# A recurrent block and a mixture-of-experts gate on one core: six blocks in a loop turn instead of two

## The chip, the core and the metric

The kernel runs on one core of one Trainium2 chip. The metric is the device time of one execution in microseconds (us). The core has five engines that run their own instruction streams: TensorE (PE, matmuls; its weight loads are shown as PEld), VectorE (DVE), ScalarE (ACT), GpSimd (POOL) and SyncE (SP), which here issues all DMA transfers. They meet through semaphores alone. The loop of this kernel is a hardware loop: every engine has its own copy of it, with its own counter and its own branch back, and no barrier joins them.

## What is computed

The input `x` is 4 batches of 4096 tokens of 512 values. After a layer normalization, two branches are computed and multiplied, and the product is added to `x`:

```python
xn = _layernorm(x)
# branch 1, on every second token: RMS norm, projection to x_proj and gate, then
def step(h, xt):
    h = jnp.tanh(h * A + xt[:, :, None] * Bm)      # h is (batch 4, 512, 64 states)
    y = h @ c_sum + Dv * xt
    return (h, y)
h_last, ys = jax.lax.scan(step, h0, x_proj)        # 2048 steps, one after the other
s = repeat((ys * silu(gate)) @ w_out.T + b_out, 2)
# branch 2, on every token: encoder 512->1024, sigmoid, controller 1024->64,
# top 2 of 8 experts (64->512->64), 64->1024, sigmoid, decoder 1024->512, layer norm
g = silu(ffn(xn))
out = x + s * g
```

All is in float32. The 2048 steps of the scan are sequential: the state after one is the input of the next.

## The kernel before, in words

The sequence is cut into 64 blocks (`NB`) of 32 steps (`STEPS`), so a block is 64 tokens of each of the 4 batches, and `LAST` is 63. The state is held as 128 partitions by 1024 columns, in two halves `f` of 512 columns. One step of the recurrence takes five kinds of instruction:

- POOL multiplies the broadcast input by `Bm` for both halves into `u`, which has two buffers (line 499, in `step` of the gpsimd function). It waits for `z_ready` of two steps earlier, and every fourth step for a chunk `xb` that SP has loaded (line 410).
- DVE multiplies the state with `A`, `ps_z = h * ps_A`, for each half (line 991), then adds `u` (line 997).
- ACT takes the tanh of each half into the ring `h` (line 601, `tanh`), and DVE's next step waits for it (`h_ready`, line 990).
- PE sums four steps at a time over the states (line 761, `y`).

All other work of a block hangs between the steps. Each engine has a table of slots (`PE_Y`, `PE_DECODE`, `ACT_RELU`, `DVE_DEC_STATS`, `POOL_FIN_SKIP` and so on): a slot of 5 is step 5 of the block itself, one under 0 lies in the block before, one of 32 or more in the block behind. `run_bodies` (line 345) goes through a block's slots and calls `steps` for the recurrence and `between` for the previous, the present and the next block. So the order on each engine is fixed by hand, and in each block an engine also finishes the one before (decoder, output) and prepares the one behind (normalization, projection). These matter below:

- `decode(blk, q)`, lines 892 and 900: the decoder's matmuls, slot 33, thus in slot 1 of the next block. DVE takes their statistics in line 1061 (`dec_stats`, slots 28.75 and 31.75), which wait for the first and the second decode.
- `experts`, lines 845, 857 and 682: expert matmuls on PE and their ReLU on ACT, which stands in ACT's queue between two tanhs.
- `gateT_copy`, line 671: one small ACT instruction in each block, at slot 12.5. It serves here as a mark of where a block is.
- `fin_skip`, line 551, is POOL's last instruction of a turn; `dec_scale`, lines 539 and 541, is POOL's scale for the decoder's norm.

Block 0 is written out, blocks 1 to 62 are 31 turns of a loop with two blocks each (line 358, `eng.Fori`), and block 63 is written out behind. Two is the least that works with buffers and semaphores that alternate by the block's parity. In the loop the number of the block stands in a register, so that counts to wait for are worked out by register instructions; in the blocks written out they are constants:

```python
with eng.Fori(0, (LAST - 1) // 2) as pair:
    body(2 * pair + 1, 1)
    body(2 * pair + 2, 0)
```

In the built program one turn has 229 instructions on SP, 208 on POOL, 460 on ACT, 566 on DVE, and on PE 584, where a matmul is counted once; the profile shows it as four records, two of PE and two of PEld. They are counted from the built program.

Of the kernel before, what the change touches and what calls it, by code (L numbers as in the profile page):

```python
# [43 lines left out]
EH = 512  # L44
T2 = 2 * P
NFILL = 34
LN_EPS = 1e-5
RMS_EPS = 1e-6

# [60 lines left out]
def build(nc, x, w_inT, b_in, A_T, B_T, Cm, Dv, w_outT, b_out, g_norm, W_enc, b_enc, W_s2c, b_s2c,  # L110
          Wr, br, W1, b1, W2, b2, W_c2s, b_c2s, W_dec, b_dec, ln_g, ln_b, out):
    NB = x.shape[1] // (2 * STEPS)
    LAST = NB - 1
# [9 lines left out]
    with ExitStack() as ctx:  # L123
# [145 lines left out]
        def fill_number(blk, k):  # L269

            if isinstance(blk, int) and blk == 0:
                return 4 + k - (2 if k >= FILL_XT else 0)
            if isinstance(blk, int) and blk == LAST:
                return NFILL * blk + 2 + k - (4 if k >= FILL_CONTE else 0)
            return NFILL * blk + 2 + k

        def fill_count(n_or_blk, k):

            if isinstance(n_or_blk, int):
                return fill_number(n_or_blk, k) // 2 + 1  # L280
            return (NFILL // 2) * n_or_blk + (2 + k) // 2 + 1

# [6 lines left out]
        def fin_fill(blk, k):  # L289

            if isinstance(blk, int) and blk == LAST:
                return None, NFILL * (LAST + 1) - 2 + k - FILL_FIN
            return blk + 1, k
# [51 lines left out]
        def run_bodies(eng, steps, between, parts=1):  # L345

            def body(blk, par):
                for n in range(STEPS * parts):
                    slot = n / parts
                    steps(blk, slot)  # L350
                    if not is_first(blk):
                        between(blk - 1, 1 - par, slot + STEPS)
                    between(blk, par, slot)
                    if not is_last(blk):
                        between(blk + 1, 1 - par, slot - STEPS)

            body(0, 0)
            with eng.Fori(0, (LAST - 1) // 2) as pair:
                body(2 * pair + 1, 1)
                body(2 * pair + 2, 0)  # L360
            body(LAST, LAST % 2)
            for n in range(STEPS * parts):
                between(LAST, LAST % 2, STEPS + n / parts)

        def is_first(blk):
            return isinstance(blk, int) and blk == 0

        def is_last(blk):
            return isinstance(blk, int) and blk == LAST
# [3 lines left out]
        def _(sp):  # L373
# [80 lines left out]
            def between(blk, par, slot):  # L454
# [10 lines left out]
                if slot == SP_STORE_OUT:  # L465
                    store_out(blk)

            run_bodies(sp, lambda blk, slot: None, between)
            sp.wait_ge(out_stored, 1 + 16 * QUAD * NB)
            sp.wait_ge(scratch_stored, 16 * QUAD * NB)  # L470
# [5 lines left out]
        def _(pool):  # L476
# [3 lines left out]
            pool.memset(minus_one[:, :], -1.0).then_inc(pool_made, 1)  # L480
            pool.memset(ln_eps[:, :], LN_EPS).then_inc(pool_made, 1)
            pool.memset(rms_eps[:, :], RMS_EPS).then_inc(pool_made, 1)
# [87 lines left out]
            def between(blk, par, slot):  # L570
# [13 lines left out]
                for q in range(2):  # L584
                    if slot == POOL_FIN_ADD[q]:
                        fin_add(blk, q)

            run_bodies(pool, step, between)

        @block.scalar
        def _(act):
# [117 lines left out]
            def between(blk, par, slot):  # L710
# [35 lines left out]
                if slot == ACT_FIN_EVAC:  # L746
                    fin_evac(blk)

            run_bodies(act, tanh, between, parts=F)

# [433 lines left out]
```

## Time and profile before

| what | value |
|---|---|
| median of 3 runs | 6597.48 us |
| lowest and highest run | 6596.17, 6603.51 us |
| span of the profiled execution | 6604.5 us |
| instructions in the profile | 111352 |
| PE, DVE, POOL, ACT busy, share of the span | 94%, 87%, 85%, 60% |
| mean granted TensorE clock, share of full speed | 0.975 |

The profiled execution's own time is not given apart from its span, from the first to the last instruction. The span lies 7.0 us above the median and 1.0 us above the slowest run. The span holds a first stretch in which the weights are loaded, and then 64 blocks of about 102 us. Busy shares are means over all of it. Register, branch and semaphore instructions are not counted as busy; an engine's sequencer that does them shows with a q behind its name (DVEq, POOLq).

### The profile page before, as it was taken

The numbers are of one execution on the slowest core, as the hardware profiler recorded it, in microseconds if no ns is written. First come the engines' busy times: TensorE is split into PE (matmuls) and PEld (weight loads), VectorE is DVE, ScalarE is ACT, GpSimd is POOL, SyncE is SP. The second block draws the span as 40 slices with busy tenths as digits, with TensorE's granted clock in tenths as the row PEclk, the third lists the DMA queues.
The fourth block names the chain that finished last, engine by engine and source line by source line (L and its number), as shares of the span: only waits on it lengthen the run. The fifth ranks groups of instructions, "written<-read, shape, count | busy, mean of one in ns | idle before, by whom it ended". The sixth has DMA issues, their size and how long they took to land.

```text
span 6604.5 us, 111352 instructions
## 1 busy us (share of the span) xinstructions
PE 6237.1 (94%) x29376; PEld 3229.9 (49%) x29376; DVE 5737.4 (87%) x10060; ACT 3984.4 (60%) x8390; POOL 5612.7 (85%) x3276
## 2 busy tenths in 40 slices
PE   5999999999999999999999999999999999999998
PEld 3554445445544454454444544445444545444454
DVE  4988889888898888988888888889888898888887
ACT  3666566566565665656656656566566665565665
POOL 4888888888888888888888888888888888888887
PEclk9999999999999999999999999999999999999999
DMA  5443444444444444444344444444444444434443
GB/s 138 104 108 92 104 109 98 106 101 101 105 98 102 100 97 106 103 97 110 93 105 101 100 106 98 103 106 96 105 101 100 106 98 103 106 95 105 103 100 83
DMA packets 158032, 675.52 MB, mean 102 GB/s; under 512 B 45589, under 2 KB 46613, under 8 KB 91799
## 3 DMA queue, kind: packets, MB, share of 16 engines
q1 hardware_dynamic: 157336, 667.24, 41.6%
q8 instruction: 315, 5.16, 0.3%
q14 instruction: 381, 3.12, 0.2%
HBM read 616.73 MB, written 50.33 MB: 101 GB/s over the span
## 4 chain that ended last, share of the span: by engine, by line
POOL 54%; issue 29%; PE 13%; DVE 1%; POOLq 1%; SPq 1%; ACT 1%; DMA 0%; DVEq 0%; ACTq 0%
POOL u L499 46%; PE bank L845 3%; POOL g L545 2%; PE ps_y L761 2%; PE ps_acc L857 2%; PE bank L794 1%; PE bank L781 1%; POOL gt L532 1%; POOL d_r L541 1%; PE bank L900 1%; PE ps_acc L900 1%; POOL conte L551 1%; PE bank L921 1%; POOL p_r L515 1%; SPq L375 1%
## 5 line engine op out<-in xcount | busy, mean ns | idle before, releaser
L499 POOL TENSOR_TENSOR u<-xb,bt 128x1024 f32<-128x1024 f32 x2048 | 4832.9, 2366 | 789.2 <-DVE ps_z L997 782.8
L601 ACT ACTIVATE h<-ps_z 128x512 f32<-128x512 f32 x4096 | 2374.7, 601 | 1691.8 <-DVE ps_z L997 1587.5
L991 DVE TENSOR_TENSOR ps_z<-h,ps_A 128x512 f32<-128x512 f32 x4096 | 2674.1, 691 | 517.3 <-ACT h L601 329.2
L997 DVE TENSOR_TENSOR ps_z<-ps_z,u 128x512 f32<-128x512 f32 x4096 | 2660.7, 691 | 39.6 <-POOL u L499 37.3
L845 PE MATMUL bank<-wide,w 65*128 65x256 f32 x4096 | 1141.2, 404 | 1.9
L761 PE MATMUL ps_y<-h,c_wide 128*32 128x512 f32 x8192 | 1007.1, 610 | 80.4 <-ACT h L601 80.4
L794 PE MATMUL bank<-xnT,w_enc 128*128 128x256 f32 x4096 | 922.4, 384 | 49.5 <-DVE g L1082 42.6
L845 PEld LDWEIGHTS bank<-wide,w 65*128 65x128 f32 x4096 | 700.2, 189 | 449.8 <-issue 320.2
L794 PEld LDWEIGHTS bank<-xnT,w_enc 128*128 128x128 f32 x4096 | 772.4, 191 | 256.9 <-issue 81.0
L682 ACT ACTIVATE hT<-bank 128x512 f32<-128x512 f32 x1024 | 604.0, 598 | 383.8 <-PE bank L845 366.4
L857 PE MATMUL ps_acc<-hT,w 128*64 128x256 f32 x4096 | 668.7, 405 | 6.6
L761 PEld LDWEIGHTS ps_y<-h,c_wide 128*32 128x32 f32 x8192 | 216.3, 110 | 615.2 <-issue 416.3
L900 PE MATMUL bank<-w_dec,wide 128*128 128x512 f32 x1024 | 480.3, 624 | 0.0
L900 PE MATMUL ps_acc<-w_dec,wide 128*128 128x512 f32 x1024 | 456.6, 599 | 0.0
L781 PE MATMUL bank<-w_in,xnT 128*128 128x512 f32 x1024 | 453.9, 597 | 0.0
L857 PEld LDWEIGHTS ps_acc<-hT,w 128*64 128x64 f32 x4096 | 202.5, 134 | 357.2 <-issue 296.8
L900 PEld LDWEIGHTS bank<-w_dec,wide 128*128 128x128 f32 x1024 | 199.1, 200 | 286.4 <-issue 286.4
L900 PEld LDWEIGHTS ps_acc<-w_dec,wide 128*128 128x128 f32 x1024 | 189.7, 190 | 262.4 <-issue 262.4
L921 PE MATMUL bank<-w_out,conte 128*128 128x512 f32 x512 | 313.9, 770 | 0.0
L624 ACT ACTIVATE wide<-bank,b_enc_col 128x256 f32<-128x256 f32 x512 | 213.9, 471 | 148.1 <-PE bank L794 148.1
L781 PEld LDWEIGHTS bank<-w_in,xnT 128*128 128x128 f32 x1024 | 191.4, 192 | 216.8 <-issue 216.5
L665 ACT ACTIVATE conte<-ps_acc,gate 128x64 f32<-128x64 f32 x1024 | 226.5, 369 | 0.0
(107 smaller groups left out, 4324.6 us busy)
## 6 DMA issues: line engine op xcount, KB each, us to landing
xb<-x_proj_scratch SPq DMA_DIRECT2D x2048, 256.0 KB, 4.3
xbuf<-in_L_attn_x SPq DMA_DIRECT2D x256, 128.0 KB
xres<-in_L_attn_x SPq DMA_DIRECT2D x512, 64.0 KB
out<-g SPq DMA_DIRECT2D x256, 128.0 KB
x_proj_scratch<-xp SPq DMA_DIRECT2D x256, 64.0 KB
w_in<-in_L_attn_w_in SPq DMA_DIRECT2D x1, 2048.0 KB
w_enc<-in_L_ffn_W_enc SPq DMA_DIRECT2D x1, 2048.0 KB
w_dec<-in_L_ffn_W_dec SPq DMA_DIRECT2D x1, 2048.0 KB
```

The costliest lines, as they stand in the source:

```text
L499: pool.tensor_tensor(u[:, tau % 2, :, :], xt, bt[:, :, :], ALU.mult).then_inc(u_ready, 1)
L601: act.activation(h[:, tau % RING, f, :], ps_z[:, f, :], ACT.Tanh).then_inc(h_ready, 1)
L682: drained(act.activation(hT[:, n % 2, :], bank[n % 2][:, :], ACT.Relu), at)
L761: ins = pe.matmul(ps_y[32 * j:32 * j + 32, :], c_wide[:, f, SP - 4 - 4 * k:2 * SP - 4 - 4 * k], h[:, (QUAD * k + j) % RING, f, :], start=( ...
L781: ins = pe.matmul(bank[half][:, :], xnT[:, par, k, 0, :], w_in[:, k, D * half:D * half + D], start=(k == 0), stop=(k == KD - 1))
L794: ins = pe.matmul(bank[n % 2][:, T2 * half:T2 * half + T2], w_enc[:, k, P * m:P * m + P], xnT[:, par, k, :, :], start=(k == 0), stop=(k == ...
L845: ins = pe.matmul(bank[n % 2][:, T2 * half:T2 * half + T2], w_1[0:MA, e, P * t:P * t + P], conteT[:, e, :], start=True, stop=True)
L857: ins = pe.matmul(eo_acc[M * half:M * half + M, :], w_2[:, 4 * (n // 2) + t, :], hT[:, n % 2, T2 * half:T2 * half + T2], start=(n == 0 and ...
L900: ins = pe.matmul(dst[:, :], wide[:, k, P * q:P * q + P], w_dec[:, k, :], start=False, stop=(k == KH - 1))
L921: ins = pe.matmul(bank[1][:, :], oT[:, k, :], w_out[:, k, :], start=False, stop=(k == KD - 1))
L991: dve.tensor_tensor(ps_z[:, f, :], h[:, (tau - 1) % RING, f, :], ps_A[:, f, :], ALU.mult).then_inc(m_done, 1)
L997: dve.tensor_tensor(ps_z[:, f, :], ps_z[:, f, :], u[:, tau % 2, f, :], ALU.add).then_inc(z_ready, 1)
```

## The change

A constant `TURN = 6` is added, and the loop holds six blocks in a turn. With `LAST` at 63 there are 62 // 6 = 10 turns, for blocks 1 to 60. Blocks 61 and 62 are then written out behind the loop, and 63 as before, so three stand there. Parities are the same as before, since 6 is even. Nothing else changes: no slot, buffer, semaphore or operation.

```diff
+TURN = 6
...
             body(0, 0)
-            with eng.Fori(0, (LAST - 1) // 2) as pair:
-                body(2 * pair + 1, 1)
-                body(2 * pair + 2, 0)
+            turns = (LAST - 1) // TURN
+            with eng.Fori(0, turns) as turn:
+                for j in range(TURN):
+                    body(TURN * turn + (1 + j), (1 + j) % 2)
+            for blk in range(TURN * turns + 1, LAST):
+                body(blk, blk % 2)
             body(LAST, LAST % 2)
             for n in range(STEPS * parts):
                 between(LAST, LAST % 2, STEPS + n / parts)
```

In the built program a turn then has 665 instructions on SP, 620 on POOL, 1372 on ACT, 1690 on DVE and 1736 on PE (a matmul again counted once). The code ahead of the loop has the same length on every engine.

PE at the end of a turn, before. Line 879 makes the inputs of the second sigmoid, 892 and 900 are the decoder, 358 is the loop.

```order
L761 MATMUL ps_y<-h,c_wide 32x512 x8
L879 MATMUL bank<-hT,w_c2s 128x256 x4
L879 MATMUL ps_acc<-hT,w_c2s 128x256 x2
L309 REGISTER_ALU
L879 MATMUL bank<-hT,w_c2s 128x256 x2
L358 REGISTER_ALU
L358 COMPARE_AND_BRANCH
```

PE in the change between the second and the third block of a turn, where the turn ended before (lines are 4 higher within the engines' functions).

```order
L765 MATMUL ps_y<-h,c_wide 32x512 x8
L883 MATMUL bank<-hT,w_c2s 128x256 x4
L883 MATMUL ps_acc<-hT,w_c2s 128x256 x2
L310 REGISTER_ALU
L883 MATMUL bank<-hT,w_c2s 128x256 x2
L760 REGISTER_ALU
L765 MATMUL ps_y<-h,c_wide 32x512 x8
L896 MATMUL bank<-bias_rows,ones 128x512
```

The order of the matmuls is the same; the loop's register instruction and branch are gone from this joint, and the sum `y` and the decoder follow at once.

DVE at the end of a turn, before. 997 adds `u`, 1061 takes the statistics of the second decode.

```order
L997 TENSOR_TENSOR ps_z<-ps_z,u 128x512
L324 REGISTER_ALU
L1061 BN_STATS d_st<-ps_acc 128x6
L358 REGISTER_ALU
L358 COMPARE_AND_BRANCH
```

DVE in the change between the second and the third block of a turn.

```order
L1001 TENSOR_TENSOR ps_z<-ps_z,u 128x512
L325 REGISTER_ALU
L1065 BN_STATS d_st<-ps_acc 128x6
L994 ISA
L995 TENSOR_TENSOR ps_z<-h,ps_A 128x512 x2
L999 ISA
```

Here too the branch is gone, and the next block's first step (995) follows behind one register instruction of another kind. The same holds for ACT, POOL and SP.

## Rows read from the trace of the kernel before

**Rows 1.** Waits of DVE: who waited for whom, us in total, times, longest.

```profile
DVE ps_z L991 <- issue: 130.9, 30, 4.9
DVE d_st L1061 <- PE bank L900: 129.6, 34, 7.7
```

**Rows 2.** Line 358 over the span: durations ns min/median/max, first and last start us.

```profile
L358 PEldq COMPARE_BRANCH  x31: 83/3934/4777, 355.0 to 6458.9; - x31
```

**Rows 3.** Line 358 in the stretch 2170 to 2220 us, the end of one turn.

```profile
L358 SPq COMPARE_BRANCH  x1: 45/45/45, 2194.5 to 2194.5; - x1
L358 SPq FUSED_REGOPS  x1: 64/64/64, 2194.8 to 2194.8; - x1
...
L358 POOLq COMPARE_BRANCH  x1: 45/45/45, 2202.3 to 2202.3; - x1
L358 POOLq FUSED_REGOPS  x1: 78/78/78, 2202.6 to 2202.6; - x1
...
L358 DVEq COMPARE_BRANCH  x1: 63/63/63, 2207.2 to 2207.2; - x1
...
L358 ACTq COMPARE_BRANCH  x1: 45/45/45, 2207.8 to 2207.8; - x1
L358 DVEq FUSED_REGOPS  x1: 85/85/85, 2212.3 to 2212.3; - x1
L358 ACTq FUSED_REGOPS  x1: 68/68/68, 2212.7 to 2212.7; - x1
```

**Rows 4.** Line 671 in four stretches: count, ns min/median/max, first and last start us.

```profile
L671 ACT ACTIVATE w<-ps_acc x61: 371/371/372, 224.9 to 6329.9; 8x256 f32<-8x256 f32 x61
L671 ACT ACTIVATE w<-ps_acc x2: 371/372/372, 224.9 to 322.8; 8x256 f32<-8x256 f32 x2
L671 ACT ACTIVATE w<-ps_acc x2: 371/371/371, 6329.9 to 6426.6; 8x256 f32<-8x256 f32 x2
L671 ACT ACTIVATE w<-ps_acc x2: 371/371/371, 6426.6 to 6524.2; 8x256 f32<-8x256 f32 x2
```

**Rows 5.** Busy us (count) of PE, PEld, DVE, ACT, POOL; clock, DMA share, GB/s.

```profile
2257.80:2354.50 96.70, 94.89 (x459) 49.63 (x459) 89.59 (x158) 62.26 (x131) 87.59 (x52) 1.00 0.45 107
2354.50:2462.90 108.40, 101.80 (x460) 51.61 (x459) 89.48 (x158) 62.20 (x132) 87.75 (x52) 0.94 0.39 96
```

**Rows 6.** Waits of PE in 2257.8 to 2354.5 us, the block without a branch.

```profile
PE bank L772 <- DVE g L1099: 1.7, 1, 1.7
```

**Rows 7.** PE in order of time around its branch: start us, us, what [idle before].

```profile
2187.49 3.36 PE L761 MATMUL ps_y<-h,c_wide 128*32 128x512 f32 x16 [2.82 <-ACT h L601]
```

**Rows 8.** PE in order of time at the same place one block earlier.

```profile
2087.88 1.92 PE L761 MATMUL ps_y<-h,c_wide 128*32 128x512 f32 x16
```

**Rows 9.** Busy us of PE (count), clock, DMA share, GB/s, just behind the branch.

```profile
2187.40:2190.60 3.20, 3.11 (x16) 0.52 0.30 98
```

**Rows 10.** DVE in order of time around its branch.

```profile
2207.61 0.69 DVE L1061 BATCH_NORM_STATS2 d_st<-ps_acc 128x6 f32<-128x512 f32 x1
2212.42 1.30 DVE L991 TENSOR_TENSOR ps_z<-h,ps_A 128x512 f32<-128x512 f32 x2 [4.12 <-issue]
2213.62 1.29 DVE L997 TENSOR_TENSOR ps_z<-ps_z,u 128x512 f32<-128x512 f32 x2
```

**Rows 11.** POOL in order of time around its branch.

```profile
2205.73 2.36 POOL L499 TENSOR_TENSOR u<-xb,bt 128x1024 f32<-128x1024 f32 x1
...
2208.83 2.36 POOL L499 TENSOR_TENSOR u<-xb,bt 128x1024 f32<-128x1024 f32 x1
2214.99 2.36 POOL L499 TENSOR_TENSOR u<-xb,bt 128x1024 f32<-128x1024 f32 x1 [3.79 <-DVE ps_z L997]
```

**Rows 12.** Waits of POOL in 2257.8 to 2354.5 us.

```profile
POOL u L499 <- DVE ps_z L997: 8.3, 16, 0.9
```

**Rows 13.** SP's DMA issues in order of time around its branch.

```profile
2204.72 1.82 SPq L410 DMA_DIRECT2D xb<-x_proj_scratch  x4
```

**Rows 14.** The second of two DMA queues that carry instructions: packets, MB, share.

```profile
q14 instruction: 381, 3.12, 0.2%
```

## The prediction

> **What bounds the kernel now.** I read the waits of DVE first. Two of its waits are of the same size and number: 130.9 us in 30 waits before line 991, the first step of a block, with nothing to wait for ("issue"), and 129.6 us in 34 waits for PE's decoder before its statistics [rows 1]. A loop of 31 turns branches back 30 times, so both look like a cost of the turn. The rows of the loop's line show how. The branch itself takes 0.05 to 0.06 us on SP, POOL, DVE and ACT [rows 3]. But the first instruction behind it comes at very different distances: on SP at 2194.8 after 2194.5, on POOL at 2202.6 after 2202.3, that is 0.3 us each; on DVE at 2212.3 after 2207.2, 5.1 us, and on ACT at 2212.7 after 2207.8, 4.9 us [rows 3]. PE shows it in the branch itself: 3.93 us in the median of 31, and 0.083 us in the shortest [rows 2], which I take for the last one, which isn't taken. The two engines that go on at once have the short turns, 229 and 208 instructions; those that stop have 460, 566 and PE's longest. The reading: a branch back to code that is no longer held near the engine waits some 4 to 5 us for it to be fetched.
>
> Next the price of a turn on the whole kernel, from a mark that comes once in a block [rows 4]. From block 1 to block 61 there are 61 marks, so 60 intervals in (6329.9 − 224.9) = 6105.0 us, 30 with a taken branch between the marks and 30 without: 203.5 us a pair. Intervals without a taken branch: 97.9 us (block 1 to 2), 96.7 (61 to 62) and 97.6 (62 to 63, where the loop is left by falling through its branch, and the code is otherwise that of an end of turn) [rows 4]. The middle of 96.7 and 97.9 is 97.3, so an interval with a branch takes 203.5 − 97.3 = 106.2 us, and a taken branch costs **8.9 us**.
>
> The same 8.9 us can be seen as work. DVE loses 129.6/30 = 4.3 and 130.9/30 = 4.4 us, together 8.7 [rows 1]: first it waits for a decoder that PE starts late, because PE has been held at its own branch, until 2187.49 [rows 7] and so 20 us ahead of DVE's, then it is held at its own. The two add, since DVE comes to them one after the other. PE also pays after its stop: 16 matmuls of line 761 take 3.36 us behind an idle time of 2.82 us [rows 7] against 1.92 us one block earlier [rows 8], and the granted clock behind the stop is 0.52 [rows 9], the lower of its two levels (1.2 instead of 2.4 GHz).
>
> Last, what bounds a block without a branch, since that is what the kernel is left with. There PE is busy 94.89 of 96.70 us at clock 1.00 [rows 5], and its only wait is 1.7 us [rows 6]; DVE, POOL and ACT are busy 89.6, 87.6 and 62.3 us. So such a block stands near PE's own work, and more of them in a row can't become much shorter than 96.7.
>
> **The change part by part.**
>
> 1. Branches removed. 31 turns with 30 taken branches become 10 turns with 9: 21 fewer, each at 8.9 us: **−187 us**. Bounds: if the converted intervals last 97.9, as block 1 to 2 does, a pair gives 203.5 − 97.9 = 105.6, and a branch costs 7.7: −162. If they last 96.7, 106.8 − 96.7 = 10.1: −212. I take the middle, since both kinds stand in rows.
>
> 2. Branches kept. Nine remain on DVE, PE and ACT, with the same instructions around them and the same length of code ahead of the loop. They cost what they cost now: 0.
>
> 3. New misses. POOL's turn grows from 208 to 620 instructions and SP's from 229 to 665, both beyond the 460 with which ACT is held. So at the nine branches POOL and SP will be held for some 5 us too. On POOL, held from 2202.3, the multiplication that starts at 2205.73 would start at about 2207.6, 1.9 us late. DVE is itself held until 2212.3 and needs that `u` at 2213.62 [rows 10]; the one behind it (2208.83, done by 2211.2, then by 2213) is followed by an idle time of 3.79 us in which POOL waits for DVE [rows 11]. The delay lies in that hole: 0. If the hole were gone, it would be 1.9 us nine times, +17, and at most 5.1 nine times, +46. SP's next issue behind its branch at 2194.5 comes at 2204.72 [rows 13], so 5 us lie inside 10: 0. A gain I exclude, as nothing gets shorter.
>
> 4. Code streamed on POOL and SP. What now stays near the engine for a whole turn must be fetched in every turn. DVE and ACT do this today: the second instruction queue carries 3.12 MB in 381 packets, 0.2% of the DMA engines [rows 14], and DVE's "issue" waits are 30 in all [rows 1], none for code in the middle of a turn. So 0; the other end is a rival below.
>
> 5. Blocks 61 and 62 written out: the same operations, with constants in place of register instructions. PE, which bounds a clean block, has the same matmuls: 0.
>
> Sum: −187 us. Against the profiled execution it gives a span of 6604.5 − 187 = 6417.5. The median of the runs lies 7.0 us under that span, and the difference carries over: 6597.5 − 187 = **6410 us**, 2.8% less.
>
> One rule of the Trainium skill bears on terms 3 and 4. The page "Runtime: NRT & Kernel Launch", section "Instruction fetch mechanics", says that instructions are kept in two blocks and fetched ahead in sequence, mostly hidden, and that a taken branch out of the window stalls. By its figures, 512 instructions for most engines, 208 and 229 stay inside and 566 does not, which agrees with rows 3, but ACT's 460 should not stall and its row shows 4.9 us. For POOL and SP at 620 and 665 it foretells the new misses of term 3, and no stall in term 4; the sum by it is the same.
>
> **The rivals.**
>
> - The new misses show. POOL, at 5 us behind on its branch, is late for DVE, or SP is late with a chunk. Against it stand the holes of 3.79 and 10 us; for it that DVE and ACT wait for one another in ways that one row doesn't show. Price: 5 to 10 us at nine branches, 45 to 90 us less gain: 6455 to 6500.
> - Slower than before: POOL stalls within the turn. If code for POOL isn't fetched in time when it runs straight on, POOL stops at every packet of code. If the 381 packets [rows 14] are those of DVE and ACT, whose 31 turns of 1026 instructions and code outside the loop come to over 32000, a packet holds some 85 or more, a turn of 620 is 5 to 7 packets, and with the blocks behind the loop there are about 60 in all. Each stop would be about 5 us, of which POOL's slack against DVE, at most 0.9 us in a clean block [rows 12], hides one part: 4.1 us by 60 is 246 us, which gives 6597 − 187 + 246 = 6656. It decides from 187/4.1 = 46 such stops on. Against it: DVE, with a turn of 566 instructions, has no such stop in 31 turns.
> - PE's clock. A core that is no longer interrupted keeps PE 98% busy for six blocks in place of two, and the clock might be granted lower. At the 0.94 of an interval with a branch, a clean block's 94.9 us would be 101, 6 us more; for the 21 converted intervals that is +126: 6536. For it: the stretches seen so far are of three blocks at most. Against it: 1.00 in the clean block, and 0.52 only right behind a stop [rows 5, 9].
> - No change. The 8.9 us might belong to every second block's work and not to the branch: 6597. Against it is the interval from block 62 to 63, the same place without a taken branch, with 97.6 us [rows 4]. A page of the Trainium skill points this way: "Advanced Engine Details and Errata", section "Control Flow Timing", gives about 108 ns for a compare-and-branch and names no fetch. By that alone 21 branches would be worth 2 us. The rows agree on the branch and disagree on what follows it.
>
> **How the numbers follow.** The forecast has a chance of 0.80, the new misses that show 0.10, the lower clock 0.03, POOL's stops 0.04, no change and others 0.03. The predicted time is the forecast's, 6410. Its own bounds are 6597 − 212 = 6385 and 6597 − 162 + 17 = 6452; the range is taken to 6460, which takes in the start of the first rival, and leaves out the others. A measurement of this kernel can tell about 0.2%, 13 us, from no change. Faster: the forecast, the first rival and the clock, 0.93. Same: 0.02. Slower: 0.05.
>
> **What would show it.** Right: DVE's "issue" waits before the first step of a block fall to 9, with some 4.4 us each, and its waits for the decoder to about 9; intervals of 96.7 to 97.9 us in 53 of 62 places and 104 to 108 in nine; mean clock up from 0.975 to about 0.99; POOL and SP now about 5 us from their branch to the next instruction, with no new wait of DVE for `u`. Wrong: intervals of clean blocks above 98 us behind the second one of a turn; waits of DVE for `u` of more than 1 us at the nine branches; "issue" waits of POOL in the middle of a turn; a granted clock under 0.97 in a clean block.

## The result, and the profile after

| | before | six blocks in a turn |
|---|---|---|
| median | 6598.35 us (4 runs) | 6422.97 us (4 runs) |
| lowest, highest | 6596.17, 6603.51 | 6419.40, 6426.32 |
| span of the profiled execution | 6604.5 | 6421.4 |
| mean granted TensorE clock | 0.975 | 0.983 |

The ratio is 0.9731, with a 95% interval of 0.9717 to 0.9745. The medians differ by 175.4 us, 2.7%. The forecast was 6410 us in a range of 6385 to 6460.

Waits of DVE after (who waited for whom, us in total, times, longest), which answer to [rows 1]. Line numbers within the engines' functions are 4 higher than before.

```profile
DVE ps_z L995 <- ACT h L605: 333.2, 585, 2.8
...
DVE ps_z L1001 <- POOL u L503: 46.5, 91, 8.8
...
DVE d_st L1065 <- PE bank L904: 38.0, 13, 7.4
DVE ps_z L995 <- issue: 37.3, 9, 4.4
```

The "issue" waits fell from 30 to 9, at 4.1 us each instead of 4.4, and the waits for the decoder from 129.6 us to 38.0. Together that is 185.2 us of waiting gone, close to the gain of the span, 183.1 us. DVE's other waits moved less: for ACT from 329.2 to 333.2 us, for POOL from 37.3 to 46.5, and for PE's line 921 (now 925) from 76.8 to 65.4. None of the waits for POOL lies at one of the nine branches: from 2 us before DVE's branch to 25 us behind it there is none in any of the nine.

The loop's line after, at the end of its first turn (720 to 775 us; durations ns min/median/max, first and last start us), which answers to [rows 3].

```profile
L360 PEldq COMPARE_BRANCH  x1: 3795/3795/3795, 740.8 to 740.8; - x1
...
L360 SPq COMPARE_BRANCH  x1: 59/59/59, 753.1 to 753.1; - x1
L360 SPq FUSED_REGOPS  x1: 64/64/64, 757.0 to 757.0; - x1
...
L360 POOLq COMPARE_BRANCH  x1: 50/50/50, 758.1 to 758.1; - x1
L360 POOLq FUSED_REGOPS  x1: 78/78/78, 760.6 to 760.6; - x1
...
L360 DVEq COMPARE_BRANCH  x1: 63/63/63, 763.0 to 763.0; - x1
...
L360 ACTq COMPARE_BRANCH  x1: 45/45/45, 763.6 to 763.6; - x1
L360 DVEq FUSED_REGOPS  x1: 85/85/85, 768.1 to 768.1; - x1
L360 ACTq FUSED_REGOPS  x1: 68/68/68, 768.7 to 768.7; - x1
```

PE, DVE and ACT stop as before, for 3.8, 5.1 and 5.1 us. POOL and SP, which went on after 0.3 us before, now stop too: POOL 2.5 us, SP 3.9 us.

POOL at that branch in order of time (start us, us, what, idle before), which answers to [rows 11].

```profile
760.33 1.26 POOL L555 TENSOR_TENSOR conte<-xp,dv_all 128x512 f32<-128x512 f32 x1
761.55 2.36 POOL L503 TENSOR_TENSOR u<-xb,bt 128x1024 f32<-128x1024 f32 x1
...
764.66 2.35 POOL L503 TENSOR_TENSOR u<-xb,bt 128x1024 f32<-128x1024 f32 x1
770.78 2.36 POOL L503 TENSOR_TENSOR u<-xb,bt 128x1024 f32<-128x1024 f32 x1 [3.77 <-DVE ps_z L1001]
```

POOL's engine sees nothing of its sequencer's stop here. The stop is over at 760.6, while the engine is busy with the old turn's last instruction (line 555) until 761.59. Later it waits 3.77 us for DVE, as before (3.79).

Busy us and count of PE, PEld, DVE, ACT and POOL, granted clock, DMA share and GB/s, in three stretches between marks of line 675 (line 671 before): an interval with a branch, a clean one behind it, and the last one. They answer to [rows 5].

```profile
813.60:910.30 96.70, 94.91 (x459) 49.57 (x459) 89.59 (x158) 62.27 (x132) 87.57 (x52) 1.00 0.43 107
708.50:813.60 105.10, 98.54 (x460) 50.74 (x459) 89.52 (x158) 62.22 (x132) 87.75 (x52) 0.97 0.40 99
6242.30:6342.20 99.90, 91.49 (x436) 47.37 (x435) 87.63 (x152) 59.68 (x128) 87.25 (x45) 0.93 0.41 98
```

The marks themselves, over the first turn and over all from block 1 on (count, ns, first and last start us), answer to [rows 4].

```profile
L675 ACT ACTIVATE w<-ps_acc x6: 371/371/372, 221.1 to 708.5; 8x256 f32<-8x256 f32 x6
L675 ACT ACTIVATE w<-ps_acc x63: 371/371/372, 221.1 to 6342.2; 8x256 f32<-8x256 f32 x63
```

Five clean intervals in a row take 487.4 us, 97.5 each. All 62 intervals take 6121.1 us. At 97.3 for each clean one and 99.9 for the last, the nine with a branch come to (6121.1 − 99.9 − 52 × 97.3)/9 = 106.8 us. Read one by one, the marks give the same: 52 clean intervals of 96.7 to 97.9 us, and nine of 103.4 to 109.7 with a mean of 106.6, where before 30 of 103.1 to 110.5 had a mean of 106.2. So a taken branch costs about as much as before.

### The profile page after: what moved, and what is told of

Read it like the earlier page. It is cut to its first block, busy times and chain, and to the rows that moved or that the text cites. A ratio compares the mean times of both kernels' runs of the same rounds, so it can differ in the third digit from the quotient of the medians.

```text
span 6421.4 us, 110057 instructions
## 1 busy us (share of the span) xinstructions
PE 6180.3 (96%) x29376; PEld 3211.1 (50%) x29376; DVE 5739.9 (89%) x10060; ACT 3988.3 (62%) x8390; POOL 5611.4 (87%) x3276
## 4 chain that ended last, share of the span: by engine, by line
PE 39%; POOL 37%; issue 19%; DVE 2%; ACT 1%; SPq 1%; POOLq 1%; DMA 0%; DVEq 0%; ACTq 0%
POOL u L503 31%; PE bank L849 8%; PE ps_y L765 6%; PE bank L798 6%; PE ps_acc L861 4%; PE bank L785 3%; PE ps_acc L904 3%; PE bank L904 3%; POOL g L549 2%; PE bank L925 1%; PE bank L883 1%; PE bank L837 1%; DVE ps_z L1001 1%; POOL gt L536 1%; POOL conte L555 1%
## 5 line engine op out<-in xcount | busy, mean ns | idle before, releaser
L995 DVE TENSOR_TENSOR ps_z<-h,ps_A 128x512 f32<-128x512 f32 x4096 | 2675.8, 691 | 428.1 <-ACT h L605 333.2
L1001 DVE TENSOR_TENSOR ps_z<-ps_z,u 128x512 f32<-128x512 f32 x4096 | 2661.7, 692 | 48.6 <-POOL u L503 46.5
L765 PE MATMUL ps_y<-h,c_wide 128*32 128x512 f32 x8192 | 993.7, 603 | 24.2 <-ACT h L605 24.2
L904 PE MATMUL bank<-w_dec,wide 128*128 128x512 f32 x1024 | 465.5, 608 | 0.0
```

Of the source, the lines that this page charges most:

```text
L765: ins = pe.matmul(ps_y[32 * j:32 * j + 32, :], c_wide[:, f, SP - 4 - 4 * k:2 * SP - 4 - 4 * k], h[:, (QUAD * k + j) % RING, f, :], start=( ...
L904: ins = pe.matmul(dst[:, :], wide[:, k, P * q:P * q + P], w_dec[:, k, :], start=False, stop=(k == KH - 1))
L995: dve.tensor_tensor(ps_z[:, f, :], h[:, (tau - 1) % RING, f, :], ps_A[:, f, :], ALU.mult).then_inc(m_done, 1)
L1001: dve.tensor_tensor(ps_z[:, f, :], ps_z[:, f, :], u[:, tau % 2, f, :], ALU.add).then_inc(z_ready, 1)
```

## The experiments

Each engine has its own loop, so each can get its own number of blocks in a turn, and its own prefetch hint, with every other engine left as it was. That makes it possible to take the stops away engine by engine. Each ratio is to executions of before that were measured beside the run, with medians of 6600.44, 6595.47 and 6596.38 us. Ratios and intervals come from all executions of both kernels, and differences in us are differences of medians, so the two can differ by some us.

**One engine's loop at six blocks.** `run_bodies` gets the number as an argument; the engines that aren't named keep two.

```diff
-        def run_bodies(eng, steps, between, parts=1):
+        def run_bodies(eng, steps, between, parts=1, TURN=2):
...
-            run_bodies(pe, lambda blk, slot: None, between)
+            run_bodies(pe, lambda blk, slot: None, between, TURN=6)
```

PE alone at six:

> Only PE's loop holds six blocks; POOL, SP, ACT and DVE keep two. My theory: a turn's price of 8.9 us is the sum of PE's stop (4.3 us, seen as DVE's wait for the decoder) and DVE's stop (4.4 us). PE then stops 9 times instead of 30, so 21 x 4.3 = 90 us are gained: about 6508 us, and DVE's 'issue' waits stay at 30 while its waits for the decoder fall to about 9. Rival, the stops are no sum but the larger of two parallel ones: about 6598, no gain. Rival, PE's stop is the whole cause and DVE's one lies in its shadow: about 6420.

Measured: 6488.24 us, ratio 0.9827 (0.9811 to 0.9844), 112 us below the 6600.44 of before. That is 5.3 us for each of 21 branches, more than the 4.3 I had for PE. DVE's waits:

```profile
DVE ps_z L994 <- issue: 116.0, 30, 4.4
...
DVE d_st L1064 <- PE bank L903: 45.6, 12, 7.7
```

DVE's "issue" waits stay at 30 and its waits for the decoder fall to 12. Both rivals fall: the gain is neither nothing nor all.

DVE alone at six, the same edit in DVE's call:

> Only DVE's loop holds six blocks. Sum of stops as I counted them: 21 x 4.4 = 92 us less, about 6506 us. Rival that I now find likelier: ACT's stop of 5.2 us begins 0.6 us behind DVE's and was covered by it; with DVE's gone, DVE waits for ACT's tanh in its place, and the gain is near nothing: 6585 to 6605 us, with waits of DVE for ACT (line 601) of 3 to 5 us in 21 places.

Measured: 6564.05 us, ratio 0.9935 (0.9918 to 0.9952): 36 us, or 1.7 us a branch. The four executions lie between 6548.90 and 6578.35, and the interval reaches from 32 to 54 us, so this is the least certain of the prices. DVE at the end of the first turn of before's length, in order of time:

```profile
378.19 1.28 DVE L994 TENSOR_TENSOR ps_z<-h,ps_A 128x512 f32<-128x512 f32 x2
379.38 1.29 DVE L1000 TENSOR_TENSOR ps_z<-ps_z,u 128x512 f32<-128x512 f32 x2
380.57 0.74 DVE L1085 SCALAR_TENSOR_TENSOR g<-bank,d_r,ln_b_all 128x512 f32<-128x512 f32 x1
383.70 0.69 DVE L994 TENSOR_TENSOR ps_z<-h,ps_A 128x512 f32<-128x512 f32 x1 [2.38 <-ACT h L604]
```

and ACT's branch there (loop's line in the stretch 350 to 390 us):

```profile
L359 ACTq COMPARE_BRANCH  x1: 45/45/45, 377.8 to 377.8; - x1
L359 ACTq FUSED_REGOPS  x1: 68/68/68, 382.9 to 382.9; - x1
```

DVE does one more step, and then stands for ACT, whose own stop of 5.1 us had lain under DVE's. So ACT's stop takes most of the place, though not all: neither number of mine, 92 or nothing, was right. The waits of 3 to 5 us for ACT that I had expected didn't come; the longest is 3.0.

PE and DVE at six:

> PE's and DVE's loops hold six blocks, ACT, POOL and SP two. If ACT's stop steps into DVE's place: 90 us less, about 6508 us, as with PE alone. If the stops of PE and DVE are all there is: about 6423 us, as the change. If POOL's and SP's new stops in the change cost something, this would come out below 6423.

Measured: 6457.25 us, ratio 0.9784 (0.9767 to 0.9800): 143 us. The two alone gave 112 and 36, so within the noise these two add up. The time lies between the two that I had expected: ACT steps into DVE's place, but only in part.

ACT, PE and DVE at six:

> ACT's, PE's and DVE's loops hold six blocks, POOL and SP two, so that these two have no stops as in the change. If the new stops of POOL (2.5 us) and SP (4 us) at nine branches of the change lie in holes, the time is that of the change, 6423 us within 6. If they show, it is 10 to 60 us less.

Measured: 6421.86 us, ratio 0.9725 (0.9709 to 0.9742), against 6422.97 for the change: the same. ACT adds 35 us, 1.7 a branch, and the stops of POOL and SP cost nothing that can be measured: the executions here lie between 6412.84 and 6425.37 us, those of the change between 6419.40 and 6426.32. DVE and ACT together, on top of PE, are worth 6488.24 − 6421.86 = 66.4 us, 3.2 a branch.

POOL and SP alone at six:

> Only POOL's and SP's loops hold six blocks, PE, DVE and ACT keep two. POOL and SP get 9 stops each where they had none, and fetch their code in every turn. If all of that is hidden: 6598 us, the same as before within 0.2%. If their stops or the streaming show: 20 to 60 us more.

Measured: 6591.92 us, ratio 0.9995 (0.9983 to 1.0007): no difference. The second instruction queue carries 526 packets here where it was 381 [rows 14], so POOL and SP do fetch their code again in every turn. So neither the nine new stops nor the streaming of POOL's and SP's code through the turn shows, from this side too.

POOL and SP at four, a single execution:

> POOL's and SP's loops hold four blocks (some 414 and 447 instructions), the others two. ACT stops with 460 instructions, POOL and SP don't with 208 and 229. If what is held near an engine is what decides, the limit lies between: POOL and SP may go on after 0.3 us each or stop for 2.5 and 4 us as at six blocks. The time stays at 6598 within 15 us either way.

Measured: 6595.57 us. Around the loop's line, 520 to 640 us:

```profile
L359 SPq COMPARE_BRANCH  x1: 59/59/59, 567.7 to 567.7; - x1
L359 SPq FUSED_REGOPS  x1: 64/64/64, 572.6 to 572.6; - x1
...
L359 POOLq COMPARE_BRANCH  x1: 50/50/50, 573.6 to 573.6; - x1
L359 POOLq FUSED_REGOPS  x1: 78/78/78, 576.3 to 576.3; - x1
```

```diff
-            with eng.Fori(0, turns) as turn:
+            with nc.Fori(0, turns, engines=OrderedEngineSet([eng.engine]),
+                         hint_back_edge=True) as turn:
```

Two blocks in a turn, hint on all engines:

> Two blocks in a turn as before, with one instruction more at the head of each engine's turn that tells the sequencer where the turn's last branch will go. If the stop behind a branch is the fetch of code that isn't at hand, it goes although all 30 branches stay: DVE's 'issue' waits of 4.4 us vanish, and the time is 30 x 8.9 = 267 us below before, about 6332 us, perhaps 5 to 15 us more for what is left of each. If the price belongs to the branch, to the registers of the loop or to every second block's work, the time stays at 6598.

Measured: 6348.66 us, ratio 0.9617 (0.9600 to 0.9635), 247 us below before with all 30 branches in place. The loop's line over the span, and at the end of the first turn:

```profile
L361 PEldq COMPARE_BRANCH  x31: 88/557/1953, 352.9 to 6200.8; - x31
```

```profile
L361 DVEq COMPARE_BRANCH  x1: 90/90/90, 372.7 to 372.7; - x1
L361 DVEq BRANCH_PREFETCH_HINT  x1: 39/39/39, 373.2 to 373.2; - x1
...
L361 ACTq COMPARE_BRANCH  x1: 68/68/68, 373.4 to 373.4; - x1
L361 ACTq BRANCH_PREFETCH_HINT  x1: 31/31/31, 373.9 to 373.9; - x1
```

DVE and ACT are on their way 0.5 us behind their branch, and PE's median is 0.56 us where it was 3.93. DVE has no "issue" wait left before its first step. This is the run that settles the cause. The profile has 155 instructions more than before's 111352, which is one hint for each of 31 turns on five engines; all else in the code is that of before, and only the knowledge where the branch will go is new.

The two instruction queues say what the stops were. Here:

```profile
q8 instruction: 286, 4.69, 0.3%
q14 instruction: 323, 2.65, 0.1%
```

and before (q14 stands in [rows 14]):

```profile
q8 instruction: 315, 5.16, 0.3%
```

With the hint q8 carries 29 packets less and q14 58 less. With the hint on PE alone it is q8 that falls to 286, with the hint on ACT and DVE alone it is q14 that falls to 323, and the other stays as it was. So q8 is PE's, and each of the 30 stops of PE, of DVE and of ACT goes together with about one packet of code that with the hint needn't be fetched. The price was the fetch.

Six blocks with the hint:

> The change with the same hint on all engines. If the stops are fetches: nine of them go, 9 x 8.9 = 80 us below the change, about 6343 us, and the same as two blocks with hints within 10 us, since then the number of blocks in a turn has no price. If not: 6423.

Measured: 6348.28 us, ratio 0.9617 (0.9599 to 0.9635). With the hint, six blocks in a turn give nothing over two.

No loop at all:

> All 64 blocks written out, no loop on any engine. By the price of a turn, 30 taken branches at 8.9 us less than before: 6598 - 267 = 6331 us; by the price that the change showed, 175/21 = 8.35 us each, 6598 - 250 = 6348. Rival, an uninterrupted PE gets a lower clock: the granted clock of clean blocks under 0.97 and a time above 6380. Rival, a stream of 16 times as much code makes engines stop for it in the middle: 'issue' waits in DVE and POOL, time above 6400.

Measured: 6344.30 us, ratio 0.9612 (0.9594 to 0.9630), the fastest, 4 us below the hinted loops. DVE's waits have no "issue" row at a step of the recurrence, and the mean clock is 0.988, so both rivals fall. The edit removes the loop:

```diff
-            with eng.Fori(0, (LAST - 1) // 2) as pair:
-                body(2 * pair + 1, 1)
-                body(2 * pair + 2, 0)
+            for blk in range(1, LAST):
+                body(blk, blk % 2)
```

**Each stop by itself.** With 6344 to 6349 us as the time without stops, the hint on some engines alone prices those of the others.

> Two blocks in a turn, the hint on ACT and DVE only, so PE alone stops, 30 times. With no stops at all the kernel takes 6345 us. Theory now: PE bounds a clean block, so its stop costs its own 4.1 us and the matmuls at the lower clock behind it, about 7 us as in the marks of the run with DVE alone at six: 6345 + 30 x 7.1 = 6558 us. My recorded term for PE (4.3 us) would give 6345 + 129 = 6474. What PE alone saved with DVE and ACT still stopping (112/21 = 5.3 us) would give 6504.

Measured: 6509.56 us, ratio 0.9868 (0.9845 to 0.9891). Against the mean of the three kernels without stops (6348.66, 6348.28 and 6344.30), 6347, PE's 30 stops cost 162.5 us, **5.4 us** each, which agrees with the 5.3 of PE alone at six. The marks had misled me to 7.1.

> Two blocks in a turn, the hint on PE only, so DVE and ACT stop 30 times each at nearly the same moment. Marks of the run with PE alone at six give 3.2 us over a clean block for such a stop: 6345 + 30 x 3.2 = 6441 us. My recorded term for DVE (4.4 us) would give 6477. If the two prices of this run and the one with PE's stops alone add up to more than 8.4 us a turn, the stops overlap in part.

Measured: 6441.34 us, ratio 0.9764 (0.9741 to 0.9787): the stops of DVE and ACT together cost 94 us, **3.1 us** each, as expected, and as the 3.2 from the loops at six. The two prices add up to 8.5 us; before against the same 6347 gives (6596 − 6347)/30 = 8.3. The seven executions of before here lie between 6581.54 and 6611.94 us, which is 1.0 us a branch, so an overlap of 0.2 us can't be told from none. The sum of the two places holds within that.

Two groups of PE's matmuls in these two kernels (busy us, mean ns, then idle before) begin to tell where PE's 5.4 us come from. PE stopping, ACT and DVE hinted:

```profile
L767 PE MATMUL ps_y<-h,c_wide 128*32 128x512 f32 x8192 | 1016.8, 615 | 81.0 <-ACT h L607 77.3 <-issue 3.7
L906 PE MATMUL bank<-w_dec,wide 128*128 128x512 f32 x1024 | 477.2, 621 | 0.0
```

PE hinted, ACT and DVE stopping:

```profile
L767 PE MATMUL ps_y<-h,c_wide 128*32 128x512 f32 x8192 | 986.5, 599 | 4.4 <-ACT h L607 4.3
L906 PE MATMUL bank<-w_dec,wide 128*128 128x512 f32 x1024 | 456.6, 599 | 0.0
```

The same matmuls take 30.3 + 20.6 = 50.9 us more where PE stops, 1.7 us a stop. Beside that, PE's engine is idle for 81.0 − 4.4 = 76.6 us more before line 767, its first matmuls behind the branch. The profile puts this wait down to ACT, but it is PE's own stop, since it goes with the hint. The whole of PE, first with the hint on all engines, then with PE stopping, then with ACT and DVE stopping:

```profile
PE 6152.4 (97%) x29376; PEld 3203.1 (50%) x29376; DVE 5741.4 (90%) x10060; ACT 3984.2 (63%) x8390; POOL 5610.8 (88%) x3276
PE 6232.7 (96%) x29376; PEld 3222.7 (50%) x29376; DVE 5738.8 (88%) x10060; ACT 3981.4 (61%) x8390; POOL 5615.2 (86%) x3276
PE 6155.2 (96%) x29376; PEld 3203.3 (50%) x29376; DVE 5737.1 (89%) x10060; ACT 3984.5 (62%) x8390; POOL 5612.4 (87%) x3276
```

The spans are 6348.3, 6507.7 and 6439.6 us. Where PE stops, its matmuls take 80.3 us longer and it is idle for 79.1 us more: 2.7 and 2.6 us a stop, together the 159.4 us by which the spans differ. Where ACT and DVE stop, its matmuls take 2.8 us longer and it is idle for 88.5 us more, 3.0 us a stop. The mean granted clock is 0.987, 0.975 and 0.987. So the stops of DVE and ACT don't lower it; PE's do, and half of what a stop of PE costs is the lower clock.

## Why the prediction was right

**The cause.** A taken branch to code that has to be fetched again: right. The hint removes the price and leaves the branches. "No change" is refuted by the result and by this run. It fits the sizes too: the same branch on POOL and SP stops with 414 instructions and more and not with 229 and less. The 108 ns that the Trainium skill's page "Advanced Engine Details and Errata", section "Control Flow Timing", gives for a compare-and-branch are of the order of the branch's own record (45 to 63 ns on four engines in [rows 3]) and leave out what follows it.

**Term 1, 21 branches at 8.9 us.** The mechanism and the count were right, the size a little high: 175.4/21 = 8.35 us. The step that was mis-sized is the last of the sum, "the difference carries over". The spans differ by 183.1 us, 4 less than 187. But the execution profiled before was slow for its kernel, 6604.5 against a median of 6598.35, while that of the change has a span 1.6 us below its median: 183.1 − 6.15 − 1.57 = 175.4. An execution of before that is 6 us slow says nothing of the one of the change, and the 7.0 us shouldn't have been carried over. The price of 8.9 us was read from that slow execution too. Of the 4 us that the spans miss, 2.3 went in the last interval, 99.9 us where it was 97.6, at a clock of 0.93. In the kernels with no loop and with hints the last interval is 99.7 to 100.1 us too; why is open. The ratio's interval reaches from 168 to 187 us, so the forecast lies at its edge.

**The two places.** I split the 8.9 us into 4.3 for PE and 4.4 for DVE by DVE's waits, and took ACT's stop as hidden at no cost. The sum holds and the split doesn't: PE is 5.4 us and DVE and ACT together 3.1. DVE's waits show how long DVE stood, not what PE lost. PE's stop costs the lower clock as well, which I had seen in [rows 7, 8, 9] and hadn't put into the split. With only ACT and DVE stopping, DVE's "issue" waits are 112.6 us, 3.8 each, and the kernel loses 3.1, so a part of them is made up. That it is made up because PE bounds a clean block is my reading and isn't shown by a run. Of the 3.1 us, DVE's loop frees 1.7, and ACT's another 1.7 once DVE's is gone; the sum is a little over 3.1, within the noise of the first. "They cost what they cost now" was right for the nine that are left: 6423 against 6347 is 76 us, 8.4 each.

**Term 3, new misses of POOL and SP.** They came, as forecast, at 2.4 to 2.8 us on POOL and 2.8 to 4.9 on SP rather than 5, and cost nothing: the run without them is the same within 1 us, and before with nothing but them added is the same within its interval. POOL's delay of 1.9 us, that I let lie in the hole of 3.79, doesn't even reach its engine at the branch shown. The Trainium skill's page "Runtime: NRT & Kernel Launch", section "Instruction fetch mechanics", had these misses right in direction. Read as a size alone, as I read it in the prediction, its 512 instructions would let POOL at 414 and SP at 447 go on, and they stop. The page speaks of a window of two blocks, and no run here varied where a loop's code lies, so whether the window would explain it is open.

**Term 4, streaming.** Right: no "issue" wait of DVE, POOL or ACT within a turn, and with no loop at all the 64 blocks run through without one. That refutes the rival in which POOL stalls inside the turn.

**PE's clock.** The rival that a PE without pauses gets a lower clock is refuted: 1.00 in the clean interval above, and the mean rises, 0.975, 0.983, 0.988, as the stops go. For the change I had named about 0.99; the 0.983 falls short of it as PE still stops nine times: six blocks with the hint have 0.987.

**What was left.** The change takes 21 of 30 stops; the other nine are 76 us, and the hint or a written-out program removes these too.

## What to carry to other kernels

Where a hardware loop's body is larger than what an engine holds of its code, every turn pays a fetch at the branch, on each engine by itself: here at 414 instructions on POOL, 447 on SP and 460 on ACT. Look for a first instruction of the turn that waits for nothing, at equal distances, and for a branch record of some us on PE. A prefetch hint at the head of the turn took it away here without longer code (6349 us), where six blocks in a turn only divided it (6423). What such a stop costs is found by taking it away on one engine at a time, because waits that were counted on another engine gave the sum well here and the shares badly.

## What the runs showed of the hardware beside that

- Over all runs, a taken branch to code that isn't held takes 3.5 to 5.1 us on PE (in its branch record), and from branch to next instruction 3.9 to 6.3 on DVE, 3.8 to 5.9 on ACT, 2.8 to 5.6 on SP, and only 2.4 to 2.8 on POOL. I can't say why POOL's is shorter.
- POOL and SP hold a loop of 208 and 229 instructions and not one of 414 and 447.
- With the hint and two blocks in a turn a branch takes 0.5 to 0.6 us on DVE and 0.4 to 0.5 on ACT; on PE it is 0.56 in the median and up to 1.95.
- A stop of 4 us on PE can be followed by matmuls at about half the clock, 3.36 us for 16 that take 1.92. At the first branch of the change it wasn't: the same 16 took 1.92 behind an idle time of 2.41 us. There the lower clock came later in the same interval: 0.77 from 785 to 800 us, where eight matmuls of line 925 took 6.66 us against 3.70 in the clean interval behind it. That this makes the intervals with a branch spread from 103 to 110 us isn't shown.
